# Rank-16 corrections on TensorE's row groups: 80 columns of the third chunk move from row groups 2 and 3 to 0 and 1, behind a semaphore

## The chip, the core and the metric

The kernel runs on one core of one Trainium2 chip. The metric is the device time of one execution in microseconds (us); the time before is the median of three runs. The profiles are of one further execution each, taken by the hardware profiler.

## The reference, cut to what matters

4096 tokens (128 batches of 32) of 512 features go through two layers. Each batch picks its own rank-16 adapter by an index.

```
# layer 0, for batch b with adapter i = itok_B_2_6[b], F = 1376
gate = x @ W_gate.T + 0.5 * (x @ A_gate[i].T) @ B_gate[i].T
up   = x @ W_up.T   + 0.5 * (x @ A_up[i].T)   @ B_up[i].T
act  = silu(gate) * up
down = act @ W_down.T + 0.5 * (act @ A_down[i].T) @ B_down[i].T
x    = x + down @ sign(weight).T + bias0
# layer 1, for batch b with adapter j = itok_B_4_50[b]
x    = x + ffn1(cond1(x, A[j], B[j]))      # linear, with low-rank parts
```

The change is in the terms `(x @ A[i].T) @ B[i].T` of gate and up, 1376 columns each, contracted over 16 ranks.

## The kernel before, in words

**Tiling.** The tokens are worked in 32 steps of 128 tokens, which are 4 batches of 32. A step is software-pipelined: step g computes gate and up of tile g, the down product of tile g-1 (`prev`) and layer 1 of tile g-2 (`pp`). Gate and up are cut into three chunks of columns, `CHUNKS`: the narrow one of 352, and two of 512. Each chunk has two PSUM banks, one for gate and one for up: `GU_BANK = [(4, 5), (0, 1), (2, 3)]`. The big products run in the full 128x128 array in split precision (three products for one).

**The rank-16 products.** They have a contraction of only 32 rows (two batches of 16 ranks), and an output of 64 tokens (the same two batches), so each uses a tile of 32 rows and 64 columns of TensorE's array. The array has four row groups of 32 rows, and two halves of 64 columns: eight such tiles. Index n (0 or 1) is the pair of batches and picks the half of 64 columns; r (0 to 3) is the row group, and the operands have to lie in the partitions of that row group. `b_rows` holds the adapters' B: in row groups 0 and 1 the gate and up parts of the first chunk (352 columns) and behind it those of the second chunk (512); in row groups 2 and 3 only the third chunk's 512 columns at that second place. `lhs_sb` holds the small left operands, and `lhs2_sb` its rows of groups 0 and 1 copied into the partitions of groups 2 and 3.

`first_rows` (L910) issues, per n, a layer-1 product into `out_ps` (L894, row group 2, 512 columns), a down correction into `y_ps` (L898, row group 3, 512 columns), and gate and up of the narrow chunk (L918, row groups 0 and 1, 352 columns). Its last product raises the semaphore `first_mm`. `second_rows` (L922) issues, per n, four products of 512 columns (L927): the second chunk's gate and up on row groups 0 and 1, the third chunk's on 2 and 3. Its last raises `second_mm`.

**What sets the order.** The program of each engine is written out by hand and runs in that order, with semaphores between engines. In `step` (L932) TensorE runs gate and up of the three chunks, the small products in between, then `first_rows`, `second_rows`, then `down` (L836, 33 products of 128x512) for the tile before, and then the next step. ScalarE (ACT) waits for `first_mm` before the narrow chunk's silu and for `second_mm` before the other two (L464). Step 0 has no `out_ps`, `y_ps` or `down` products, step 1 has no `out_ps` products. `load_b` (L322) brings `b_rows` of the next tile on SyncE's queue (SP), 4 transfers a step.

Each fp32 product here appears as two passes in the trace: 8 products of L927 per step times 32 steps are 256, and the trace has 512. The two passes of a product are called A and B below.

Of the kernel before, what the change touches and what calls it, by code (L numbers as in the profile page):

```python
# [18 lines left out]
CHUNKS = [(1024, 352), (0, 512), (512, 512)]  # L19
# [14 lines left out]
T_AT, TD_AT, T1_AT = 0, T_W, T_W + TD_W  # L34
SMALL = T_W + 2 * TD_W
LORA_ROWS = 4 * RANK
PAIR = CHUNKS[0][1] + CHUNKS[1][1]
ROW = 3 * 512
LINE = 512
GU_BANK = [(4, 5), (0, 1), (2, 3)]  # L40
# [35 lines left out]
PAIRS = GB // 2  # L76


def build_adaln_ffn(nc, xT, x, wgu, signT, wd, bd, btab, atab, la, lbw, w1T, a1, b1tab, b1end,
                    bias, ids, consts, sb_table, c_table, out):  # L80
    ctx = ExitStack()
    with ctx:

        base = (nc.sbuf_base + LINE - 1) // LINE * LINE
        cursor = [base]

        def place(name, shape, dtype, at=None, line=LINE):
            n = 4 * int(np.prod(shape[1:]))
            n = (n + line - 1) // line * line
            if at is None:  # L90
                at = cursor
            t = nc.alloc_sbuf_tensor_at(name, shape, dtype, offset=at[0])
            at[0] += n
            return t
# [15 lines left out]
        lhs_sb = place("lhs_sb", [P, P], f32)  # L110
        lhs2_sb = place("lhs2_sb", [P, P], f32)
        loop_at = [cursor[0]]
        b_rows = place("b_rows", [P, PAIRS, PAIR], f32)
        cs_rows = place("cs_rows", [P, PAIRS, H], f32)
# [7 lines left out]
        actT_sb = place("actT_sb", [P, NBLK, 2, P], f32r)  # L122
        ad_raw = place("ad_raw", [P, GB, ADW], f32)
        b1_raw = place("b1_raw", [P, GB, KC * RANK], f32)
        cursor[0] += 12288
        loop_end = cursor[0]
        bias_sb = place("bias_sb", [P, 2, H], f32)
        const_sb = place("const_sb", [P, CONST_W], f32, line=32)
# [40 lines left out]
        def bank(name):  # L169
            return ctx.enter_context(nc.psum_tensor(name, [P, 512], f32))  # L170

        gu_ps = [bank(f"gu{n}_ps") for n in range(6)]
# [7 lines left out]
        def sem(name):  # L180
            return ctx.enter_context(nc.semaphore(name))
# [14 lines left out]

        names = ("xT_in", "xT_hi", "xT_lo", "xT_used", "x_in", "x_biased", "x1_done", "x1_turned", "x1T_in", "x1_biased",
                 "out_done", "stored", "a_in", "ad_moved", "b1_in", "b_in", "c_in", "sbd_in", "small_mm", "small_scaled",
                 "lhs_ready", "lhs2_in", "first_mm", "second_mm", "y_mm", "silu_done", "act_done", "act_turned",
                 "act_in0", "act_in1", "act_in2", "actT_hi", "actT_lo")  # L200
        L = {n: sem(n) for n in names}
        names = ("x1_half", "x1_tr", "x1_raw", "b1_in", "c_in", "lhs_ready", "x1_biased")
# [35 lines left out]
        def group(r):  # L238

            return slice(r * QUAD, (r + 1) * QUAD)  # L240
# [5 lines left out]
        def pair(n):  # L246

            return slice(n * 2 * SEQ, (n + 1) * 2 * SEQ)
# [546 lines left out]
        def _(pe):  # L795
# [9 lines left out]
            def gate(g, c, pieces=range(KC)):  # L805
                f, w = CHUNKS[c]
                if 0 in pieces:
                    if c == 0:
                        if first(g):
                            pe.wait_ge(S["wg_lo"], KC)  # L810
                        pe.wait_ge(L["xT_lo"], g + 1)
                    if not first(g):
                        pe.wait_ge(L["act_done"], g * NC - NC + c + 1)
                product(gu_ps[GU_BANK[c][0]][:, 0:w], [(xT_sb[:, k, a, :], wg_sb[:, b, k, f:f + w])
                                                       for k in pieces for a, b in THREE], None,
                        start=0 in pieces, stop=KC - 1 in pieces)

            def up(g, c, pieces=range(KC)):
                f, w = CHUNKS[c]
                if 0 in pieces and first(g):  # L820
                    pe.wait_ge(S["wu_lo"], (c + 1) * KC)
                last = product(gu_ps[GU_BANK[c][1]][:, 0:w], [(xT_sb[:, k, a, :], wu_sb[:, b, k, f:f + w])
                                                              for k in pieces for a, b in THREE], None,
                               start=0 in pieces, stop=KC - 1 in pieces)
                if c == NC - 1 and KC - 1 in pieces:
                    last.then_inc(L["xT_used"], 1)

            def down(g, c, to=y_ps, blocks=range(4), begin=False):
                if 0 in blocks:
                    pe.wait_ge(L["actT_lo"], g * NC + c + 1)  # L830
                count = len(CHUNK_BLOCKS[c])
                for n, blk in enumerate(CHUNK_BLOCKS[c]):
                    if n not in blocks:
                        continue
                    for a, b in THREE:
                        last = nc.tensor.matmul(to[:], actT_sb[:, ACTT_SLOT[c] + n, a, :], down_sb[:, blk, b, :],  # L836
                                                start=begin and (c, n) == (0, 0) and (a, b) == (0, 0),
                                                stop=c == NC - 1 and n == count - 1 and (a, b) == (1, 0),
                                                skip_group_check=True)
                return last  # L840
# [30 lines left out]
            def small_ready(g, prev, pp):  # L871
                pe.wait_ge(L["a_in"], 16 * GB * (g + 1))
                if first(g):
                    pe.wait_ge(S["down_lo"], NBLK)
                if prev is not None:
                    pe.wait_ge(L["act_in0"], SENT * g)
                    pe.wait_ge(L["act_in1"], SENT * g)
                    pe.wait_ge(L["act_in2"], SENT * g)
                    pe.wait_ge(L["ad_moved"], g)
                if pp is not None:  # L880
                    pe.wait_ge(L["x1T_in"], SENT * (pp + 1))
                    pe.wait_ge(L["b1_in"], 16 * GB * (pp + 1))
                    after(pe, L["out_done"], pp)

            def small(prev, pp):
                last = t_rows()
                if prev is not None:
                    last = td_rows()
                if pp is not None:
                    last = t1_rows(b1_raw)  # L890
                last.then_inc(L["small_mm"], 1)
# [9 lines left out]
            def lora_ready(g, prev, pp):  # L901
                pe.wait_ge(L["lhs2_in"], g + 1)
                pe.wait_ge(L["b_in"], 16 * GB * (g + 1))
                if prev is not None:
                    pe.wait_ge(L["sbd_in"], 16 * GB * g)
                    after(pe, L["x1_done"], prev)
                if pp is not None:
                    pe.wait_ge(L["c_in"], 16 * GB * (pp + 1))

            def first_rows(prev, pp):  # L910
                w = CHUNKS[0][1]
                for n in range(PAIRS):
                    if pp is not None:
                        out_rows(n)
                    if prev is not None:
                        down_rows(n)
                    for u in range(2):
                        last = nc.tensor.matmul(gu_ps[GU_BANK[0][u]][pair(n), 0:w], lhs_sb[group(u), pair(n)],  # L918
                                                b_rows[group(u), n, 0:w], start=False, stop=True, skip_group_check=True)
                last.then_inc(L["first_mm"], 1)  # L920

            def second_rows():  # L922
                for n in range(PAIRS):
                    for r in range(4):
                        c, u = 1 + r // 2, r % 2
                        lhs = lhs_sb if c == 1 else lhs2_sb
                        last = nc.tensor.matmul(gu_ps[GU_BANK[c][u]][pair(n), :], lhs[group(r), pair(n)],  # L927
                                                b_rows[group(r), n, CHUNKS[0][1]:PAIR], start=False, stop=True,
                                                skip_group_check=True)
                last.then_inc(L["second_mm"], 1)  # L930

            def step(g, prev, pp):  # L932
                gate(g, 0)
                up(g, 0)
                gate(g, 1)
                up(g, 1, range(0, 1))
                small_ready(g, prev, pp)
                up(g, 1, range(1, 2))
                small(prev, pp)
                up(g, 1, range(2, 4))  # L940
                gate(g, 2)
                up(g, 2, range(0, 3))
                lora_ready(g, prev, pp)
                up(g, 2, range(3, 4))
                first_rows(prev, pp)
                second_rows()
                if prev is not None:
                    for c in range(NC):
                        down(prev, c).then_inc(L["y_mm"], 1)
# [95 lines left out]
            for n, blk in enumerate(BLOCK_ORDER):  # L1045
# [5 lines left out]
                else:  # L1051
                    pe.wait_ge(S["down_lo"], n - 3)
                product(ring_ps[(KC + 10 + n) % 4][:], [(half[:, k, at], sign_sb[:, k, :])
                                                             for k in range(KC) for half in (wd_hi, wd_lo)],
                        S["down_mm"])
            step(0, None, None)
            step(1, 0, None)
            step(2, 1, 0)
            with pe.Fori(3, G - 1) as g:
# [62 lines left out]
```

## Time and profile before

| | |
|---|---|
| Runs | 904.69, 906.72, 906.94 us; median 906.72 us |
| Profiled execution, span from the first to the last instruction | 904.5 us; its own time is given only by this span |
| TensorE matmul (PE) busy | 896.3 us, 99% of the span |
| TensorE weight load (PEld) busy | 723.2 us |
| VectorE (DVE), ScalarE (ACT), GpSimd (POOL) busy | 411.8, 200.6, 100.2 us |
| Chain that ended last | PE 94% |
| One step of the loop | 26.15 us |

In the profile's rows, a time is in microseconds from the span's start, and L with a number is the line of the kernel. PE is TensorE's matrix products, PEld its loading of weights, which overlaps PE. The end of a matmul is modelled: it lies later than the moment at which the last column went in. "Idle before" is the time an engine sat idle, and behind the arrow stands what released it. SPq and ACTq are the DMA queues of SyncE and ScalarE.

### The profile page before, as it was taken

How to read it: one execution, taken by the hardware profiler on the slowest of the kernel's cores; microseconds unless marked ns; L12 is line 12 of the kernel's file. 1: busy time of each engine (PE TensorE's matmuls, PEld its weight loads, DVE VectorE, ACT ScalarE, POOL GpSimd, SP SyncE). 2: the span in 40 equal slices, each digit the busy share in tenths (PEclk: the TensorE clock that was granted, in tenths of full speed). 3: DMA queues.
4: the chain of work that ended last, by engine and by line, in shares of the span. 5: the costliest groups of instructions: out<-in, count | busy, mean ns of one | idle time of the engine just before them, and what ended most of it. 6: DMA issues, size and time to landing. Idle time of an engine off the chain costs nothing.

```text
span 904.5 us, 25718 instructions
## 1 busy us (share of the span) xinstructions
PE 896.3 (99%) x9487; PEld 723.2 (80%) x9487; DVE 411.8 (46%) x1021; ACT 200.6 (22%) x349; POOL 100.2 (11%) x79
## 2 busy tenths in 40 slices
PE   8999999999999999999999999999999999999998
PEld 5887788778888887888888788888887888888775
DVE  5853435444353444534444444353544434444444
ACT  4852212112112111111212212121211211211110
POOL 0200111010111110101111010111100011111011
PEclk9999999999999999999999999999999999999999
DMA  9925454554554455545455555554555545445533
GB/s 336 418 97 146 122 144 132 147 141 138 144 145 135 129 147 147 142 131 152 131 135 143 148 141 133 151 136 139 133 146 144 142 136 148 134 133 144 148 109 88
DMA packets 147413, 134.71 MB, mean 149 GB/s; under 512 B 53312, under 2 KB 118848, under 8 KB 147264
## 3 DMA queue, kind: packets, MB, share of 16 engines
q1 hardware_dynamic: 92160, 108.59, 41.5%
q10 hardware_dynamic: 54288, 22.70, 9.7%
q0 software_dynamic: 944, 3.15, 0.9%
q8 instruction: 13, 0.21, 0.1%
q14 instruction: 8, 0.07, 0.0%
HBM read 92.14 MB, written 11.01 MB: 114 GB/s over the span
## 4 chain that ended last, share of the span: by engine, by line
PE 94%; SPq 2%; DMA 1%; issue 1%; DVE 1%; ACT 0%; DVEq 0%; ACTq 0%
PE gu_ps L799 54%; PE y_ps L836 26%; PE gu_ps L927 3%; PE out_ps L856 3%; PE out_ps L894 2%; PE out_ps L845 1%; PE y_ps L799 1%; PE out_ps L866 1%; PE out_ps L799 1%; PE gu_ps L918 1%; SPq L256 1%; DMA a_raw<-in_a 1%; SPq L313 0%; SPq L343 0%; SPq L350 0%
## 5 line engine op out<-in xcount | busy, mean ns | idle before, releaser
L799 PE MATMUL gu_ps<-wu_sb,xT_sb 128*128 128x512 f32 (+1 forms) x1152 | 261.4, 371 | 0.5 <-DMA landed<-act_sb 0.3
L799 PE MATMUL gu_ps<-wg_sb,xT_sb 128*128 128x512 f32 (+1 forms) x1152 | 251.9, 367 | 0.4 <-DVE act_sb L620 0.4
L836 PE MATMUL y_ps<-down_sb,actT_sb 128*128 128x512 f32 x1023 | 241.6, 393 | 0.0
L836 PEld LDWEIGHTS y_ps<-down_sb,actT_sb 128*128 128x128 f32 x1023 | 189.6, 188 | 64.0 <-issue 25.2
L799 PEld LDWEIGHTS gu_ps<-wg_sb,xT_sb 128*128 128x128 f32 x1152 | 206.9, 188 | 31.6 <-DVE xT_sb L602 1.3
L799 PEld LDWEIGHTS gu_ps<-wu_sb,xT_sb 128*128 128x128 f32 x1152 | 204.3, 188 | 30.1 <-issue 1.2
L602 DVE TENSOR_TENSOR actT_sb<-landed,actT_sb 128x512 fp32r<-128x512 f32 (+1 forms) x96 | 61.5, 642 | 198.6 <-ACT actT_sb L455 198.6
L455 ACT CAST actT_sb<-landed 128x512 fp32r<-128x512 f32 (+1 forms) x96 | 56.1, 585 | 307.7 <-issue 273.1
L643 DVE STREAM_TRANSPOSE lhs_sb<-t_own 32x32 f32<-32x32 f32 x512 | 103.9, 203 | 7.7
L425 POOL TENSOR_TENSOR x_in<-x_in,bias_sb 128x512 f32<-128x512 f32 x32 | 41.4, 1293 | 592.8 <-DMA x_in<-in_x 592.8
L602 DVE TENSOR_TENSOR xT_sb<-xT_raw,xT_sb 128x512 fp32r<-128x512 f32 x32 | 22.1, 692 | 124.7 <-ACT xT_sb L455 124.7
L429 POOL TENSOR_TENSOR x_sb<-x_sb,bias_sb 128x512 f32<-128x512 f32 x31 | 51.2, 1651 | 166.4 <-DVE x_turn L655 166.4
L634 DVE TENSOR_TENSOR t_own<-out_ps,const_sb 128x128 f32<-128x128 f32 (+3 forms) x35 | 9.8, 280 | 124.4 <-PE out_ps L866 119.6
L624 DVE STREAM_TRANSPOSE act_sb<-act_sb 128x512 f32<-128x512 f32 (+1 forms) x96 | 64.1, 667 | 3.3
L620 DVE TENSOR_TENSOR act_sb<-act_sb,gu_ps 128x512 f32<-128x512 f32 (+1 forms) x96 | 58.0, 604 | 0.2 <-ACT act_sb L466 0.2
L455 ACT COPY ad_raw<-a_raw 128x704 f32<-128x704 f32 x32 | 25.0, 782 | 146.3 <-PE out_ps L866 139.4
L466 ACT ACTIVATE act_sb<-gu_ps 128x512 f32<-128x512 f32 (+1 forms) x96 | 49.7, 552 | 29.0 <-PE gu_ps L918 19.5
L927 PE MATMUL gu_ps<-b_rows,lhs_sb 32*64 32x512 f32 x512 | 42.6, 588 | 0.0
L455 ACT CAST xT_sb<-xT_raw 128x512 fp32r<-128x512 f32 x32 | 19.8, 620 | 94.3 <-PE gu_ps L799 94.3
L894 PE MATMUL out_ps<-cs_rows,lhs_sb 32*64 32x512 f32 (+1 forms) x128 | 34.5, 606 | 0.0
L898 PE MATMUL y_ps<-cs_rows,lhs_sb 32*64 32x512 f32 x124 | 33.9, 613 | 0.0
L856 PE MATMUL out_ps<-ad_raw,landed 128*32 128x16 f32 x2816 | 31.4, 185 | 0.0
(121 smaller groups left out, 475.1 us busy)
## 6 DMA issues: line engine op xcount, KB each, us to landing
b_rows<-in_btab SPq DMA_DIRECT2D x128, 216.0 KB
a_raw<-in_atab SPq DMA_DIRECT2D x128, 152.0 KB, 2.4
landed<-act_sb SPq DMA_DIRECT2D x132, 64.0 KB, 2.1
xT_raw<-in_xT SPq DMA_DIRECT2D x32, 256.0 KB, 2.6
x_in<-in_x SPq DMA_DIRECT2D x32, 256.0 KB, 2.8
landed<-act_sb ACTq DMA_DIRECT2D x124, 64.0 KB, 2.2
x_landed<-x_turn ACTq DMA_DIRECT2D x124, 64.0 KB, 2.2
out_x<-out_sb SPq DMA_DIRECT2D x31, 256.0 KB, 2.9
```

The costliest lines, as they stand in the source:

```text
L429: nc.gpsimd.tensor_tensor(x1_sb[:], x1_sb[:], bias_sb[:, 1, :], ALU.add).then_inc(L["x1_biased"], 1)
L455: return nc.scalar.copy(o, i)
L466: nc.scalar.activation(act_sb[c][:, 0:w], gu_ps[GU_BANK[c][0]][:, 0:w], ACT.Silu).then_inc(L["silu_done"], 1)
L602: return nc.vector.tensor_tensor(o, whole, hi(high), ALU.subtract)
L620: nc.vector.tensor_tensor(a, a, gu_ps[GU_BANK[c][1]][:, 0:w], ALU.mult).then_inc(L["act_done"], 1)
L624: nc.vector.transpose(act_sb[c][:], act_sb[c][:]).then_inc(L["act_turned"], 1)
L643: turned = nc.vector.transpose(lhs_sb[group(group_of[r]), tokens(b)], wide[tokens(b), :])
L799: last = nc.tensor.matmul(o, w, m, start=start and n == 0, stop=stop and n == len(terms) - 1, skip_group_check=not check)
L836: last = nc.tensor.matmul(to[:], actT_sb[:, ACTT_SLOT[c] + n, a, :], down_sb[:, blk, b, :], start=begin and (c, n) == (0, 0) and (a, b) == ...
L856: last = nc.tensor.matmul(small_ps[tokens(b), TD_AT:TD_AT + TD_W], landed[c][:, at:at + SEQ], ad_raw[:, b, blk * RANK:(blk + 1) * RANK], s ...
L894: return nc.tensor.matmul(to[pair(n), at], lhs_sb[group(r), pair(n)], cs_rows[group(r), n, at], start=True, stop=True, skip_group_check=True)
L927: last = nc.tensor.matmul(gu_ps[GU_BANK[c][u]][pair(n), :], lhs[group(r), pair(n)], b_rows[group(r), n, CHUNKS[0][1]:PAIR], start=False, s ...
```

## The change

`HEAD` is 432 and `TAIL` is 80. The third chunk's last 80 columns of gate and up are stored behind the second chunk's in row groups 0 and 1 of `b_rows`, which grows from 864 to 944 columns (`PAIR`); the free space behind the loop's tiles shrinks by 512 bytes per partition. Four new products (`tail_rows`) compute these 80 columns on row groups 0 and 1, between `first_rows` and `second_rows`. They write the banks that the third chunk's products of row groups 2 and 3 write. Therefore the last of them raises a new semaphore `tail_mm`, for which TensorE itself waits. `second_rows` now issues the second chunk's four products first, then waits, then issues the third chunk's four, of 432 columns.

```diff
-PAIR = CHUNKS[0][1] + CHUNKS[1][1]
+HEAD = 432
+TAIL = CHUNKS[2][1] - HEAD
+LOW = CHUNKS[0][1] + CHUNKS[1][1]
+PAIR = LOW + TAIL
...
-        cursor[0] += 12288
+        cursor[0] += 11776
...
-            def second_rows():
+            def tail_rows():
+
                 for n in range(PAIRS):
-                    for r in range(4):
-                        c, u = 1 + r // 2, r % 2
-                        lhs = lhs_sb if c == 1 else lhs2_sb
-                        last = nc.tensor.matmul(gu_ps[GU_BANK[c][u]][pair(n), :], lhs[group(r), pair(n)],
-                                                b_rows[group(r), n, CHUNKS[0][1]:PAIR], start=False, stop=True,
+                    for u in range(2):
+                        last = nc.tensor.matmul(gu_ps[GU_BANK[2][u]][pair(n), HEAD:HEAD + TAIL],
+                                                lhs_sb[group(u), pair(n)], b_rows[group(u), n, LOW:PAIR],
+                                                start=False, stop=True, skip_group_check=True)
+                last.then_inc(L["tail_mm"], 1)
+
+            def second_rows(g):
+                w = CHUNKS[0][1]
+                for n in range(PAIRS):
+                    for u in range(2):
+                        nc.tensor.matmul(gu_ps[GU_BANK[1][u]][pair(n), :], lhs_sb[group(u), pair(n)],
+                                         b_rows[group(u), n, w:LOW], start=False, stop=True, skip_group_check=True)
+                pe.wait_ge(L["tail_mm"], g + 1)
+                for n in range(PAIRS):
+                    for u in range(2):
+                        last = nc.tensor.matmul(gu_ps[GU_BANK[2][u]][pair(n), 0:HEAD], lhs2_sb[group(2 + u), pair(n)],
+                                                b_rows[group(2 + u), n, w:w + HEAD], start=False, stop=True,
                                                 skip_group_check=True)
                 last.then_inc(L["second_mm"], 1)
...
                 first_rows(prev, pp)
-                second_rows()
+                tail_rows()
+                second_rows(g)
...
             to = 0 if c == 0 else CHUNKS[0][1]
+            if c == 2:
+                b_rows[:, u, :, LOW:PAIR] = part[:, :, f + HEAD:f + w]
+                w = HEAD
             b_rows[:, u + (2 if c == 2 else 0), :, to:to + w] = part[:, :, f:f + w]
```

The new lines move the numbers of the lines behind them: L894 becomes L897, L898 L901, L918 L921, L836 L839; the tail products stand in L929, the second chunk's in L938 and the third's in L943.

TensorE (PE), in the loop's body, from the first of `first_rows` to the first `down` product, before:

```order
L894 MATMUL out_ps<-cs_rows,lhs_sb 64x512
L898 MATMUL y_ps<-cs_rows,lhs_sb 64x512
L918 MATMUL gu_ps<-b_rows,lhs_sb 64x352 x2
L894 MATMUL out_ps<-cs_rows,lhs_sb 64x512
L898 MATMUL y_ps<-cs_rows,lhs_sb 64x512
L918 MATMUL gu_ps<-b_rows,lhs_sb 64x352 x2
L927 MATMUL gu_ps<-b_rows,lhs_sb 64x512 x8
L830 ISA
L836 MATMUL y_ps<-down_sb,actT_sb 128x512 [waits actT_lo]
```

The same place after the change:

```order
L897 MATMUL out_ps<-cs_rows,lhs_sb 64x512
L901 MATMUL y_ps<-cs_rows,lhs_sb 64x512
L921 MATMUL gu_ps<-b_rows,lhs_sb 64x352 x2
L897 MATMUL out_ps<-cs_rows,lhs_sb 64x512
L901 MATMUL y_ps<-cs_rows,lhs_sb 64x512
L921 MATMUL gu_ps<-b_rows,lhs_sb 64x352 x2
L929 MATMUL gu_ps<-b_rows,lhs_sb 64x80 x4
L938 MATMUL gu_ps<-b_rows,lhs_sb 64x512 x4
L943 MATMUL gu_ps<-b_rows,lhs_sb 64x432 [waits tail_mm]
L943 MATMUL gu_ps<-b_rows,lhs_sb 64x432 x3
L833 ISA
L839 MATMUL y_ps<-down_sb,actT_sb 128x512 [waits actT_lo]
```

Eight products of 512 have become four of 80, four of 512 and four of 432, and the first of the last four waits. Nothing else moved here. Step 0 on TensorE, before, with the last full-array product of `up` ahead and the next step's first behind:

```order
L799 MATMUL gu_ps<-wu_sb,xT_sb 128x512 [waits b_in,lhs2_in]
L799 MATMUL gu_ps<-wu_sb,xT_sb 128x512 x2
L918 MATMUL gu_ps<-b_rows,lhs_sb 64x352 x4
L927 MATMUL gu_ps<-b_rows,lhs_sb 64x512 x8
L799 MATMUL gu_ps<-wg_sb,xT_sb 128x352 [waits act_done,xT_lo]
```

and after the change:

```order
L802 MATMUL gu_ps<-wu_sb,xT_sb 128x512 x2
L921 MATMUL gu_ps<-b_rows,lhs_sb 64x352 x4
L929 MATMUL gu_ps<-b_rows,lhs_sb 64x80 x4
L938 MATMUL gu_ps<-b_rows,lhs_sb 64x512 x4
L943 MATMUL gu_ps<-b_rows,lhs_sb 64x432 [waits tail_mm]
L943 MATMUL gu_ps<-b_rows,lhs_sb 64x432 x3
L802 MATMUL gu_ps<-wg_sb,xT_sb 128x352 [waits act_done,xT_lo]
```

In step 0 row groups 2 and 3 have no earlier product; here too the third chunk's products now stand behind the wait.

## Rows read from the trace of the kernel before

**Rows 1.** The page: busy time by engine, and TensorE's granted clock in 40 slices.

```profile
PE 896.3 (99%) x9487; PEld 723.2 (80%) x9487; DVE 411.8 (46%) x1021; ACT 200.6 (22%) x349; POOL 100.2 (11%) x79
...
PEclk9999999999999999999999999999999999999999
```

**Rows 2.** The chain that ended last, 404 to 415 us: start, length, what.

```profile
405.80 0.86 PE gu_ps L927 x16
406.66 7.72 PE y_ps L836 x33
```

**Rows 3.** Groups by line: busy us, mean ns, idle before.

```profile
L927 PE MATMUL gu_ps<-b_rows,lhs_sb 32*64 32x512 f32 x512 | 42.6, 588 | 0.0
L927 PEld LDWEIGHTS gu_ps<-b_rows,lhs_sb 32*64 32x64 f32 x512 | 19.8, 132 | 7.3
```

**Rows 4.** Timeline, one loop step's row-group products: start, length, engine, line, count, idle before.

```profile
404.70 0.64 PE L894 MATMUL out_ps<-cs_rows,lhs_sb 32*64 32x512 f32 x1
404.71 0.64 PE L898 MATMUL y_ps<-cs_rows,lhs_sb 32*64 32x512 f32 x1
404.71 0.51 PE L918 MATMUL gu_ps<-b_rows,lhs_sb 32*64 32x352 f32 x2
...
405.18 0.59 PE L894 MATMUL out_ps<-cs_rows,lhs_sb 32*64 32x512 f32 x1
...
405.21 0.59 PE L898 MATMUL y_ps<-cs_rows,lhs_sb 32*64 32x512 f32 x1
405.36 1.30 PE L927 MATMUL gu_ps<-b_rows,lhs_sb 32*64 32x512 f32 x16
406.59 0.30 PEld L836 LDWEIGHTS y_ps<-down_sb,actT_sb 128*128 128x128 f32 x2 [0.81 <-issue]
```

**Rows 5.** Timeline of PE at 405.3 to 405.4 us: L918's B passes, L927's first.

```profile
405.06 0.49 PE L918 MATMUL gu_ps<-b_rows,lhs_sb 32*64 32x352 f32 x4
...
405.36 0.62 PE L927 MATMUL gu_ps<-b_rows,lhs_sb 32*64 32x512 f32 x4
```

**Rows 6.** Timelines of PE at 406.0 to 406.1 and 406.25 to 406.3 us.

```profile
405.61 1.05 PE L927 MATMUL gu_ps<-b_rows,lhs_sb 32*64 32x512 f32 x12
...
405.79 0.87 PE L927 MATMUL gu_ps<-b_rows,lhs_sb 32*64 32x512 f32 x8
```

**Rows 7.** Timeline, a later small product of 32 columns on 32-column weights.

```profile
422.26 0.46 PE L845 MATMUL out_ps<-a_raw,xT_raw 128*32 128x32 f32 x32
```

**Rows 8.** Timeline of ACT in the same step: the silus that wait for first_mm and second_mm.

```profile
406.00 0.46 ACT L466 ACTIVATE act_sb<-gu_ps 128x352 f32<-128x352 f32 x1 [0.52 <-PE gu_ps L918]
406.75 1.09 ACT L466 ACTIVATE act_sb<-gu_ps 128x512 f32<-128x512 f32 x2 [0.28 <-PE gu_ps L927]
```

**Rows 9.** Timeline of step 0, where no out_ps or y_ps product runs.

```profile
71.68 0.53 PE L918 MATMUL gu_ps<-b_rows,lhs_sb 32*64 32x352 f32 x4
...
72.03 0.47 PE L918 MATMUL gu_ps<-b_rows,lhs_sb 32*64 32x352 f32 x4
...
72.20 1.16 PE L927 MATMUL gu_ps<-b_rows,lhs_sb 32*64 32x512 f32 x12
...
72.57 0.46 ACT L466 ACTIVATE act_sb<-gu_ps 128x352 f32<-128x352 f32 x1
```

**Rows 10.** Timeline near the end: VectorE's step, and the weight load that waits for it.

```profile
886.95 0.65 DVE L602 TENSOR_TENSOR actT_sb<-landed,actT_sb 128x512 fp32r<-128x512 f32 x1
...
887.65 0.99 PEld L836 LDWEIGHTS gu_ps<-down_sb,actT_sb 128*128 128x128 f32 x5 [0.48 <-DVE actT_sb L602]
```

**Rows 11.** Timeline of SP's queue, and the transfers by line (KB each).

```profile
419.61 3.38 SPq L326 DMA_DIRECT2D b_rows<-in_btab  x4
...
b_rows<-in_btab SPq DMA_DIRECT2D x128, 216.0 KB
```

**Rows 12.** One step as a window: busy time and records of each engine, clock, DMA share, GB/s.

```profile
404.70:430.85 26.15, 26.15 (x290) 21.29 (x289) 11.54 (x30) 5.00 (x9) 2.94 (x2) 1.00 0.51 141
```

More of the change, by code:

```diff
@@ L198, in build_adaln_ffn @@
                  "out_done", "stored", "a_in", "ad_moved", "b1_in", "b_in", "c_in", "sbd_in", "small_mm", "small_scaled",
-                 "lhs_ready", "lhs2_in", "first_mm", "second_mm", "y_mm", "silu_done", "act_done", "act_turned",
+                 "lhs_ready", "lhs2_in", "first_mm", "second_mm", "tail_mm", "y_mm", "silu_done", "act_done", "act_turned",
                  "act_in0", "act_in1", "act_in2", "actT_hi", "actT_lo")
```

## Prediction, made before the changed kernel ran

> **What bounds the kernel now.** I read the page first: TensorE is busy for 896.3 of 904.5 us and its granted clock stands in the top tenth in every slice [rows 1], and a loop step shows clock 1.00 and TensorE busy for all of its 26.15 us [rows 12]. So no clock effect is in play, and whatever lengthens or shortens TensorE's own row of work shows in the end 1 to 1. The chain of waits says the same where the change sits: L927 runs straight into the 33 down products, with nothing between [rows 2]. By group, L927 costs 42.6 us of TensorE's time [rows 3], or 1.33 us a step. But these are up to eight products at a time, and a mean of 588 ns tells nothing of who ends last. The timeline of one step does, cut into narrow windows so that it shows the four-product groups apart.
>
> All eight tiles of the array start together at 404.70 [rows 4]. A pass goes by its columns: L918's B passes (352 columns) start at 405.06 and the next product on their row groups at 405.36 [rows 5], 0.30 us; L927 on row groups 0 and 1 starts its A passes at 405.36 [rows 5], and its B passes at 405.79 [rows 6], 0.43 us for 512 columns. Both are 0.84 ns a column. The first pass after the change of tile shape costs 0.05 us more (L894 from 404.70 to 405.18 is 0.48, against 0.43) [rows 4]: there nothing hid its weight load. So, with "in" for the moment at which the last column has gone in:
>
> - row groups 0 and 1: 352 then 512; in at 405.79 + 0.43 = 406.22.
> - row groups 2 and 3: 512 then 512; the third chunk's A passes start at 405.61 [rows 6], and are in at 405.61 + 0.86 = 406.47. They end last, 0.25 us behind the others.
>
> The down products' weights start at 406.59 [rows 4], 0.12 us after that. This switch of tile shape stays.
>
> **The change part by part.**
>
> *Columns.* Groups 2 and 3 lose 80 columns per n, in two passes: 160 x 0.84 = 0.13 us. Groups 0 and 1 gain them: tail A passes at 405.36, B at 405.43, the second chunk's A at 405.50, its B at 405.93, in at 406.36. An 80-column pass (0.067 us) must also hide the next weight load. What a load occupies is less than the 0.13 us of its record [rows 3]: L845's 32 passes over four column tiles take 0.46 us, of which about 0.2 is the last one's modelled tail, so 8 per tile in 0.26, 0.03 us for 32 columns of weights [rows 7]; 64 columns are then some 0.05 to 0.06, just under 0.067. If a load did occupy all its 0.13 us, each of the two tail passes would last 0.06 us longer, and groups 0 and 1 would be in at 406.49; by the next point they still don't end last. I cost this at nothing.
>
> *The wait.* This is the term that decides. Without it the columns alone would bring the end from 406.47 to 406.36, 0.11 us a step. The third chunk's first weight load may now start only when `tail_mm` has been seen. When is that? The last tail pass starts about 405.46 and its record would end 0.07 + 0.16 us later (0.16 is a record's length less its columns: 0.59 - 0.43), at 405.69. But a semaphore of TensorE seems to be raised in program order, after every earlier product is complete. `first_mm` shows it. It hangs on L918's last, whose records end at 405.06 + 0.49 = 405.55 [rows 5], and ScalarE, idle for 0.52 us and waiting for just that, starts only at 406.00 [rows 8]: 0.45 us later. In step 0, where L894 and L898 don't run, L918's records end at 72.03 + 0.47 = 72.50 and ScalarE starts at 72.57 [rows 9]: 0.07 us. For `second_mm` it is 406.75 [rows 8] less 405.36 + 1.30 = 406.66 [rows 4]: 0.09 us. What is issued ahead of L918's last and ends behind it is L898's B pass on the other half, at 405.21 + 0.59 = 405.80 [rows 4]. From there to 406.00 is 0.20 us, of which some is ScalarE's own step before its instruction. `tail_mm` stands behind the same L898, and eight more passes. So the signal can't come before 405.80, and TensorE's waking adds what it does elsewhere: VectorE ends at 887.60 and the weight load starts at 887.65 [rows 10], 0.05 us. Bounds: 405.80 + 0.09 = 405.89 if it is as prompt as `second_mm`, and 406.00 + 0.08 = 406.08 if it is later than ScalarE's start on `first_mm` by 0.01 us for each of the eight tail passes behind. I take 405.98, nearer to what `first_mm` shows, since the same backlog stands ahead of it.
>
> The Trainium skill (TensorE: Matmul & The Clock Gate, Part 3, "The mechanism") says that matmuls start and end strictly in program order. By this trace half of it fails: L918's B passes start at 405.06, ahead of L894's at 405.18 [rows 4, 5], although L894 is issued first. The half on the end is what `first_mm` shows. Taken whole, it would hold the third chunk's start until the second chunk's B passes have started, at 405.93 to 405.96, and the sum would be within 0.02 us of the same.
>
> *The third chunk's end.* Its weight load is exposed now, as for L894: 0.05 us. Then two passes of 432 columns, 0.72 us: 405.98 + 0.05 + 0.72 = 406.75, against 406.47. That is +0.28 us a step. Row groups 0 and 1, in at 406.36, wait for it. Queued behind the waiting load on TensorE are the 33 down products and the next step, all on the path; nothing gives the time back, as TensorE is idle nowhere in a step [rows 12]. The silus of the second and third chunk wait for `second_mm` and come 0.28 us later, but so does everything that uses them, so no new wait arises. The narrow chunk's silu doesn't move.
>
> *Step 0.* L918 starts at 71.68, and the second and third chunk on their tiles are in at about 71.68 + 0.05 + 0.60 + 0.86 = 73.19. After: the tail ends at 71.68 + 0.05 + 0.60 + 0.13 + 0.16 = 72.62, plus 0.09 and 0.05 to 72.76, plus 0.05 + 0.72 = 73.53: +0.34 us.
>
> *Transfers.* `b_rows` grows from 864 to 944 columns, 9%, so 216 KB becomes 236 KB, four times a step. They are issued from 419.61 to 422.99 [rows 11], and the next step's row-group products, which use them, begin at 430.85 [rows 12], 7.9 us later; 9% of a transfer of a few us, with the DMA engines at 0.51, fits in that gap: nothing. The four more products (8 more passes) add no time on TensorE's issue, as eight products started within 0.05 us of each other at 404.70.
>
> *Sum.* 31 x 0.28 + 0.34 = 9.0 us. The profiled execution's span would go from 904.5 to 913.5. The median of the runs is 2.2 us above that span, so 906.7 + 9.0 = 915.7; I give 915.5.
>
> **The rivals.**
>
> 1. *The signal comes with the tail's own completion.* Then it is at 405.69, the load starts at 405.69 + 0.09 = 405.78, and the third chunk is in at 406.55: +0.08 us a step, 2.7 us, 909.4. For it: the tail's tiles are done by then. Against it: the 0.45 us of `first_mm`, against 0.07 without the longer products.
> 2. *The balance pays: faster.* The wait is released before it binds. The third chunk is in before 406.47 only if its load starts before 405.69, and the full 0.11 us a step comes if it starts by 405.58. Then 32 x -0.11 = -3.5 us, 903.2. For it: the two pairs of row groups are unequal by 0.25 us now. Against it: the tail's records themselves end at 405.69, so even a signal without any delay gives nothing.
> 3. *TensorE drains at the wait.* The waiting load holds back until the second chunk's products are done, or these are held with it: the third chunk starts at 406.36 and is in at 407.13, +0.66 us a step, 21 us, 927.8. For it: no wait on a product that is still running in the array is in the trace. Against it: passes start ahead of earlier-issued ones on other tiles, so tiles don't hold each other back; and the second chunk is issued ahead of the wait.
> 4. *No difference*, the wait being absorbed by idle time elsewhere: there is none in a step, and this is worth 906.7.
>
> **How the numbers follow.** Forecast 0.80, rival 1 0.07, rival 2 0.03, rival 3 0.07, rival 4 0.03. The forecast's own range is from the load's start at 405.89 (+0.19, 6.1 us, 912.8) to 406.08 (+0.38, 12.1 us, 918.8). The runs before spread over 2.2 us, and so I take the range from 909.2, which lets rival 1 in, to 919.5. Left out are rivals 2, 3 and 4. A measurement here can tell about 0.3%, or 2.7 us, from no change. Rival 1 falls on that bound, and I give half of it to each side. Faster 0.03; same 0.03 + 0.04 = 0.07; slower 0.90.
>
> **What would show it.** In the changed profile: a step's period of 26.43 us in place of 26.15; the third chunk's first weight load (L943) some 1.28 us after the step's first L897 (405.98 - 404.70), where the third chunk's first pass before was at 0.91; a gap of about 0.37 us on row groups 2 and 3 between the end of L897's and L901's B passes and that start; tail passes 0.07 us apart; the first down weights at 2.17 us after the first L897, in place of 1.89; the narrow chunk's silu still 1.30 us after it. I am wrong if L943 starts at 1.08 or earlier (rival 1), if it starts only at 1.66 (rival 3), or if the down products don't move.

## The result

The changed kernel takes 914.46 us (median of 4 runs, 914.19 to 915.03), the kernel before 905.76 us in the same comparison (median of 4 runs, 904.69 to 906.94; the 906.72 us that I predicted from was the median of three of them): a ratio of 1.0098, 95% interval 1.0082 to 1.0114. It is slower by 8.7 us. A later comparison gave 914.97 against 905.96 us, 1.0099 (1.0078 to 1.0119). I predicted 915.5 us, in a range from 909.2 to 919.5.

### The profile page after: what moved, and what is told of

Same layout as the page of the kernel before. It is cut to its first block, busy times and chain, and to the rows that moved or that the text cites. A ratio compares the mean times of both kernels' runs of the same rounds, so it can differ in the third digit from the quotient of the medians.

```text
span 912.5 us, 26230 instructions
## 1 busy us (share of the span) xinstructions
PE 905.4 (99%) x9743; PEld 725.2 (79%) x9743; DVE 414.8 (45%) x1021; ACT 200.9 (22%) x349; POOL 99.9 (11%) x79
## 4 chain that ended last, share of the span: by engine, by line
PE 95%; SPq 2%; DVE 1%; issue 1%; DMA 1%; ACT 0%; DVEq 0%
PE gu_ps L802 54%; PE y_ps L839 25%; PE out_ps L859 3%; PE gu_ps L938 3%; PE out_ps L897 2%; PE gu_ps L943 2%; PE out_ps L848 1%; PE y_ps L802 1%; PE out_ps L802 1%; PE gu_ps L921 1%; PE out_ps L869 1%; SPq L259 1%; DVE act_sb L627 0%; PE gu_ps L929 0%; DVE act_sb L623 0%
## 5 line engine op out<-in xcount | busy, mean ns | idle before, releaser
L839 PE MATMUL y_ps<-down_sb,actT_sb 128*128 128x512 f32 x1023 | 241.1, 393 | 0.0
L839 PEld LDWEIGHTS y_ps<-down_sb,actT_sb 128*128 128x128 f32 x1023 | 189.6, 188 | 59.5 <-issue 21.0
L897 PE MATMUL out_ps<-cs_rows,lhs_sb 32*64 32x512 f32 (+1 forms) x128 | 34.5, 606 | 0.0
L859 PE MATMUL out_ps<-ad_raw,landed 128*32 128x16 f32 x2816 | 34.0, 186 | 0.0
L901 PE MATMUL y_ps<-cs_rows,lhs_sb 32*64 32x512 f32 x124 | 33.9, 613 | 0.0
L938 PE MATMUL gu_ps<-b_rows,lhs_sb 32*64 32x512 f32 x256 | 33.6, 587 | 0.0
```

The costliest lines, as they stand in the source:

```text
L859: last = nc.tensor.matmul(small_ps[tokens(b), TD_AT:TD_AT + TD_W], landed[c][:, at:at + SEQ], ad_raw[:, b, blk * RANK:(blk + 1) * RANK], s ...
L897: return nc.tensor.matmul(to[pair(n), at], lhs_sb[group(r), pair(n)], cs_rows[group(r), n, at], start=True, stop=True, skip_group_check=True)
L938: nc.tensor.matmul(gu_ps[GU_BANK[1][u]][pair(n), :], lhs_sb[group(u), pair(n)], b_rows[group(u), n, w:LOW], start=False, stop=True, skip_g ...
```

## The profile after

The page has TensorE as busy as before, and the clock as full [rows 1]; the step shown here takes 26.46 us, against 26.15 [rows 12] (the means over the loop's steps are 26.45 and 26.15):

```profile
span 912.5 us, 26230 instructions
...
PE 905.4 (99%) x9743; PEld 725.2 (79%) x9743; DVE 414.8 (45%) x1021; ACT 200.9 (22%) x349; POOL 99.9 (11%) x79
...
PEclk9999999999999999999999999999999999999999
```

```profile
407.66:434.12 26.46, 26.46 (x304) 21.37 (x304) 11.64 (x30) 5.00 (x9) 2.95 (x2) 1.00 0.53 142
```

The second is the window of one step, with the columns of [rows 12]. This is the same place as [rows 4], in the timeline of PE:

```profile
407.66 0.64 PE L897 MATMUL out_ps<-cs_rows,lhs_sb 32*64 32x512 f32 x1
...
408.14 0.59 PE L897 MATMUL out_ps<-cs_rows,lhs_sb 32*64 32x512 f32 x1
...
408.17 0.59 PE L901 MATMUL y_ps<-cs_rows,lhs_sb 32*64 32x512 f32 x1
408.32 0.33 PE L929 MATMUL gu_ps<-b_rows,lhs_sb 32*64 32x80 f32 x8
408.45 1.05 PE L938 MATMUL gu_ps<-b_rows,lhs_sb 32*64 32x512 f32 x8
409.00 0.95 PE L943 MATMUL gu_ps<-b_rows,lhs_sb 32*64 32x432 f32 x8
409.88 0.97 PE L839 MATMUL y_ps<-down_sb,actT_sb 128*128 128x512 f32 x3
```

and in those of the weight loads (PEld) and of ACT:

```profile
408.39 0.23 PEld L938 LDWEIGHTS gu_ps<-b_rows,lhs_sb 32*64 32x64 f32 x8
408.99 0.21 PEld L943 LDWEIGHTS gu_ps<-b_rows,lhs_sb 32*64 32x64 f32 x8 [0.37 <-PE gu_ps L929]
409.88 0.76 PEld L839 LDWEIGHTS y_ps<-down_sb,actT_sb 128*128 128x128 f32 x4 [0.68 <-issue]
```

```profile
408.96 0.47 ACT L469 ACTIVATE act_sb<-gu_ps 128x352 f32<-128x352 f32 x1 [0.52 <-PE gu_ps L921]
410.02 1.09 ACT L469 ACTIVATE act_sb<-gu_ps 128x512 f32<-128x512 f32 x2 [0.59 <-PE gu_ps L943]
```

Read from the step's first product (407.66, and 404.70 in [rows 4]): the tail's records end at 408.32 + 0.33 = 408.65, 0.99 after it, where the prediction has 405.69, also 0.99. The third chunk's first weights come at 408.99, 1.33 after it, 0.34 us behind those records. The down weights come at 2.22, against 1.89 before. The narrow chunk's silu stands where it was, at 1.30 [rows 8]. The summary of waits names the place in 31 steps:

```profile
PEld gu_ps L943 <- PE gu_ps L929: 11.5, 31, 0.4
```

Row groups 2 and 3, free at 0.91, stand still until 1.33.

## The experiments

Positions are from the step's first row-group product, a step's length is the mean over the loop's steps in the trace. Theory: a semaphore of TensorE is raised in program order, so `tail_mm` waits for the longer products issued ahead of the tail, on other row groups.

**1. The tail ahead of everything.** Nothing long stands ahead of `tail_mm` here, and the wait is kept.

```diff
-                first_rows(prev, pp)
                 tail_rows()
+                first_rows(prev, pp)
                 second_rows(g)
```

> The changed kernel with tail_rows ahead of first_rows, wait kept. Theory (TensorE's semaphore is raised in program order, behind the longer out_ps and y_ps products): nothing long stands ahead of tail_mm now, it comes about 0.45 us after the step's first product, before row groups 2 and 3 are free at 0.91; the wait costs nothing and the balanced columns pay: both pairs of row groups are in at 1.64, against 1.77 in the kernel before, step 26.02 us in place of 26.15, 31 steps x -0.13 = -4.0 us, about 901.7 us against 905.8. Rival (a wait inside the row-group products costs a fixed drain or wake of 0.3 us wherever its signal comes from): the third chunk still starts at about 1.3, step 26.4 us, about 914 us.

Measured: 901.4 us against 905.53, ratio 0.9952 (0.9938 to 0.9965); step 26.02 us. Its PE and PEld timelines:

```profile
481.28 0.30 PE L929 MATMUL gu_ps<-b_rows,lhs_sb 32*64 32x80 f32 x4
...
482.22 0.56 PE L943 MATMUL gu_ps<-b_rows,lhs_sb 32*64 32x432 f32 x4
482.49 0.61 PE L938 MATMUL gu_ps<-b_rows,lhs_sb 32*64 32x512 f32 x4
482.58 0.55 PE L943 MATMUL gu_ps<-b_rows,lhs_sb 32*64 32x432 f32 x4
```

```profile
481.79 0.17 PEld L943 LDWEIGHTS gu_ps<-b_rows,lhs_sb 32*64 32x64 f32 x4
...
483.06 0.30 PEld L839 LDWEIGHTS y_ps<-down_sb,actT_sb 128*128 128x128 f32 x2 [0.68 <-issue]
```

The waiting weights are loaded at 0.51, beside the products before them, and the third chunk starts at 0.94, as soon as its row groups are free. Both pairs are in together: 482.49 + 0.43 = 482.92 and 482.58 + 0.36 = 482.94. The wait itself costs nothing once its signal is early. The rival of a fixed price of 0.3 us falls: the trace records the rise of `tail_mm` at 0.41, and the waiting weights are loaded 0.10 us behind it.

**2. The long products behind the tail.** The tail stays behind the narrow chunk; the `out_ps` and `y_ps` products are issued after it.

```diff
                 for n in range(PAIRS):
-                    if pp is not None:
-                        out_rows(n)
-                    if prev is not None:
-                        down_rows(n)
                     for u in range(2):
...
                 first_rows(prev, pp)
                 tail_rows()
+                wide_rows(prev, pp)     # out_rows and down_rows; its last raises first_mm
                 second_rows(g)
```

> The changed kernel with the out_ps and y_ps products issued behind the narrow chunk's and the tail's, ahead of the second chunk's; first_mm is raised by the last y_ps product. Theory (program order): only the tail's own products stand before tail_mm, so it comes at their own completion, 0.985 + 0.04 = 1.03 us after the first product; the third chunk's weights start at 1.07 in place of 1.33, down weights 2.21 - 0.26 = 1.95, step 26.19 to 26.22 us, about 907 to 908.5 us. Rival (the signal was late because of something else than the out_ps and y_ps products, such as the short passes or the wait itself): third chunk still at 1.33, step 26.44 us, 914.5 us.

Measured: 905.47 us against 905.53, ratio 0.9995 (0.9986 to 1.0004); step 26.15 us. The timelines of PE and PEld:

```profile
482.92 0.53 PE L917 MATMUL gu_ps<-b_rows,lhs_sb 32*64 32x352 f32 x4
...
483.56 0.32 PE L935 MATMUL gu_ps<-b_rows,lhs_sb 32*64 32x80 f32 x8
```

```profile
483.96 0.21 PEld L949 LDWEIGHTS gu_ps<-b_rows,lhs_sb 32*64 32x64 f32 x8
484.85 0.30 PEld L839 LDWEIGHTS y_ps<-down_sb,actT_sb 128*128 128x128 f32 x2 [0.68 <-issue]
```

The tail's records end at 483.56 + 0.32 = 483.88, and the waiting weights follow 0.08 us later, at 1.04 in place of 1.33. The tail's passes are the same, at nearly the same place. Only what was issued ahead of them differs. The signal then comes with the tail's own completion. The weights stand 0.03 us ahead of what I expected, the down weights at 1.93 as expected (1.95), but the step is 0.04 to 0.07 us shorter than expected: it gives back what the place loses, behind the start of the down weights (see the end of the next section).

**3. The wait without the tail.** The kernel before, second chunk's products first, then a wait for `first_mm`, then the third chunk's, 512 columns each.

```diff
+                for c in (1, 2):
+                    if c == 2:
+                        pe.wait_ge(L["first_mm"], g + 1)
                     for n in range(PAIRS):
-                    for r in range(4):
-                        c, u = 1 + r // 2, r % 2
+                        for u in range(2):
+                            r = u + (2 if c == 2 else 0)
```

> The kernel before, columns unchanged (no tail), with the second chunk's four products issued ahead of the third's, and between them a wait of TensorE for its own first_mm. Theory (program order): the third chunk's weights start at first_mm 1.20 + 0.04 = 1.24 us, and two passes of 512 are in at 2.15 against 1.77: +0.38 us a step, step 26.53 us, +11.8 us, about 917.5 us. If the signal came with the narrow chunk's own completion (0.85 + 0.04): weights at 0.93, +0.07 us a step, 908 us. If the cost in the changed kernel came from the tail's passes and not from the wait: no change, 905.8 us.

Measured: 917.14 us against 905.53, ratio 1.0119 (1.0099 to 1.0139); step 26.48 us. The timeline of PEld:

```profile
541.93 0.13 PEld L894 LDWEIGHTS out_ps<-cs_rows,lhs_sb 32*64 32x64 f32 x1 [0.35 <-issue]
...
543.17 0.21 PEld L930 LDWEIGHTS gu_ps<-b_rows,lhs_sb 32*64 32x64 f32 x8 [0.42 <-PE gu_ps L918]
544.19 0.30 PEld L836 LDWEIGHTS y_ps<-down_sb,actT_sb 128*128 128x128 f32 x2 [0.81 <-issue]
```

The weights start at 1.24, as expected of program order, though the product that raises `first_mm` has its record's end at 0.85. So the tail isn't needed for the loss: with the late signal and the new order alone it is 11.6 us, and experiment 4 shows that the order costs nothing.

**4. The order without the wait.** The kernel before with the second chunk's four products first.

```diff
+                for c in (1, 2):
                     for n in range(PAIRS):
-                    for r in range(4):
-                        c, u = 1 + r // 2, r % 2
+                        for u in range(2):
+                            r = u + (2 if c == 2 else 0)
```

> The kernel before with the second chunk's four products issued ahead of the third's and no wait. Theory (tiles start as soon as they are free, whatever was issued ahead on other tiles): no change, step 26.15 us, 905.8 us. Rival (products start in program order): the third chunk's A passes can't start before the second chunk's B passes at 1.09 to 1.12, in place of 0.91: +0.2 us a step, step 26.35 us, about 912 us.

Measured: 906.05 us against 905.53, ratio 1.0005 (0.9993 to 1.0018); step 26.14 us, the down weights at 1.89:

```profile
535.68 0.13 PEld L894 LDWEIGHTS out_ps<-cs_rows,lhs_sb 32*64 32x64 f32 x1 [0.35 <-issue]
...
537.57 0.30 PEld L836 LDWEIGHTS y_ps<-down_sb,actT_sb 128*128 128x128 f32 x2 [0.81 <-issue]
```

That is the timeline of PEld. The one of PE, cut to 537.00 to 537.02 us, when the second chunk's A passes are over, shows the third chunk's A passes and the second chunk's B passes:

```profile
536.59 0.80 PE L928 MATMUL gu_ps<-b_rows,lhs_sb 32*64 32x512 f32 x8
```

The third chunk starts at 0.91, as before the edit, and the second chunk's B passes, issued ahead of it, can't start before 1.09. The new order costs nothing: products of different tiles start when their tile is free.

**5. The tail in twice as many products.** Each tail product of 80 columns is two of 40, so 16 passes stand between `first_mm` and `tail_mm`.

```diff
                     for u in range(2):
-                        last = nc.tensor.matmul(gu_ps[GU_BANK[2][u]][pair(n), HEAD:HEAD + TAIL],
+                        for at in (0, TAIL // 2):
+                            last = nc.tensor.matmul(gu_ps[GU_BANK[2][u]][pair(n), HEAD + at:HEAD + at + TAIL // 2],
...
```

> The changed kernel with each tail product of 80 columns split into two of 40: 16 tail passes between first_mm and tail_mm in place of 8. In the changed kernel tail_mm is raised 0.093 us after first_mm. Theory a (completions behind the long products are worked off one by one, 0.012 us a pass): tail_mm comes 0.19 us after first_mm, the third chunk's weights start at 1.42 in place of 1.33, step 26.53 us, 31 x 0.09 = 2.8 us above the changed kernel, about 917.3 us. Theory b (0.093 us is what a second semaphore costs, whatever stands between): third chunk at 1.33, step 26.44 us, 914.5 us. Under both, row groups 0 and 1 end later by 0.09 us at most and don't end last.

Measured: 915.62 us against 905.96, ratio 1.0104 (1.0083 to 1.0126); step 26.46 us. The timelines of PE and PEld:

```profile
541.66 0.59 PE L897 MATMUL out_ps<-cs_rows,lhs_sb 32*64 32x512 f32 x1
...
542.04 0.62 PE L940 MATMUL gu_ps<-b_rows,lhs_sb 32*64 32x512 f32 x1
542.05 0.24 PE L930 MATMUL gu_ps<-b_rows,lhs_sb 32*64 32x40 f32 x2
542.29 0.80 PE L940 MATMUL gu_ps<-b_rows,lhs_sb 32*64 32x512 f32 x4
```

```profile
541.18 0.13 PEld L897 LDWEIGHTS out_ps<-cs_rows,lhs_sb 32*64 32x64 f32 x1 [0.35 <-issue]
...
542.59 0.21 PEld L945 LDWEIGHTS gu_ps<-b_rows,lhs_sb 32*64 32x64 f32 x8
543.47 0.30 PEld L839 LDWEIGHTS y_ps<-down_sb,actT_sb 128*128 128x128 f32 x2 [0.68 <-issue]
```

The weights come at 1.40 in place of 1.33 (the mean over the loop's steps; the rounded rows give 542.59 - 541.18 = 1.41): eight more passes ahead of the signal cost 0.07 us, a little under 0.01 us each. That speaks for the backlog being worked off pass by pass, at less than the 0.012 us that I had. A fixed price of a second semaphore would have left 1.33. The time itself can't tell the two apart (0.65 us between the medians), and the step of 26.46 us isn't 26.53: again the rest of the step gives part of it back.

**6. The changed kernel again,** on the same chip as experiments 5 and 7.

```diff
(no edit to the changed kernel)
```

> The changed kernel as it is, on the same chip as the split one: 914.5 us against 905.5, step 26.44 us.

Measured: 914.97 us against 905.96; step 26.47 us. It reproduces.

**7. The tail first, with 48 columns.** Experiment 1 with `HEAD = 464`.

```diff
-HEAD = 432
+HEAD = 464
```

> As the kernel with tail_rows ahead of first_rows, but 48 columns moved in place of 80. Theory (the wait is free there, and columns cost 0.84 ns each): row groups 2 and 3 end last, at 0.94 + 2 x 0.39 = 1.72 against 1.66 with 80 and 1.77 before; down weights at 1.84, step 26.06 us, 902.9 us (31 x 0.05 above the 80-column version). Rival (the gain of that version comes from the new order and not from the balance): as with 80 columns, 901.4 us.

Measured: 902.26 us against 905.96, ratio 0.9957 (0.9940 to 0.9973); step 26.05 us against 26.02 of experiment 1. The timelines of PE and PEld:

```profile
482.82 0.27 PE L929 MATMUL gu_ps<-b_rows,lhs_sb 32*64 32x48 f32 x4
...
484.01 0.61 PE L938 MATMUL gu_ps<-b_rows,lhs_sb 32*64 32x512 f32 x4
484.14 0.58 PE L943 MATMUL gu_ps<-b_rows,lhs_sb 32*64 32x464 f32 x4
```

```profile
484.65 0.53 PEld L839 LDWEIGHTS y_ps<-down_sb,actT_sb 128*128 128x128 f32 x3 [0.73 <-issue]
```

Now row groups 2 and 3 end last again: 484.14 + 0.39 = 484.53 against 484.01 + 0.43 = 484.44, and the down weights come at 1.83, between 1.78 of experiment 1 and 1.89 before. In the trace the gain goes by the columns moved. In the times the two versions aren't apart, as their intervals overlap.

## Why the prediction was right, point by point

- **Which row groups end last, and 0.84 ns a column: right.** Experiments 1 and 7 place the down weights at 1.78 and 1.83 by this count. The balance was worth the 0.11 to 0.13 us a step that the columns give: 4.1 us in experiment 1.
- **The signal in program order: right.** It was argued from `first_mm` alone. Experiments 1 to 3 show it in three ways: with the tail first, with the long products behind it, and with no tail at all. Rival 1 (own completion) had the weights at 1.08; they come at 1.33, and at 1.04 only when nothing longer is issued ahead. The traces also record when each semaphore rises, and say the same directly. `first_mm` rises 0.35 us behind the end of its own product's record in a step of the kernel before (1.20 against 0.85), and 0.04 us behind it in step 0, where nothing longer is ahead. `tail_mm` rises 0.31 us behind (1.29 against 0.99) in the changed kernel, and 0.04 us behind in experiments 1 and 2. The waiting weights follow the rise by 0.04 us in the changed kernel and in experiments 2, 3 and 5.
- **The place of the signal: 0.05 us too early.** I took 405.98, that is 1.28; it is 1.33. I had counted 0.01 us for each tail pass behind `first_mm` in the upper bound, and then chosen a value below it. The backlog is near that bound: `tail_mm` rises 0.09 us after `first_mm` with 8 tail passes between them, and 0.16 us after it with the 16 of experiment 5. The bound I had set, 1.38, holds it.
- **Rival 3 (TensorE drains at the wait): wrong.** The third chunk's weights start at 408.99, while the second chunk's records run to 408.45 + 1.05 = 409.50. Its B passes start at 408.88, so that their last columns go in at 408.88 + 0.43 = 409.31, also behind that load.
- **Rival 2 (the balance pays): not in this order.** Its decision point was right: the load has to start before 0.99. Experiment 1 meets it, and is faster.
- **Step 0: wrong, +0.34 us predicted, nothing measured.** The third chunk is held as predicted: its weights start at 71.81, 1.05 after the first L921 at 70.76, where I had 1.08. But in step 0 nothing follows but the next step's gate product, and that waits for VectorE, which works on the narrow chunk. Before and after, in the timelines of step 0:

```profile
73.10 0.51 DVE L620 TENSOR_TENSOR act_sb<-act_sb,gu_ps 128x352 f32<-128x352 f32 x1
...
73.76 1.05 PE L799 MATMUL gu_ps<-wg_sb,xT_sb 128*128 128x352 f32 x5 [0.40 <-DVE act_sb L620]
```

```profile
70.76 0.82 PE L921 MATMUL gu_ps<-b_rows,lhs_sb 32*64 32x352 f32 x8
...
71.81 0.59 PE L943 MATMUL gu_ps<-b_rows,lhs_sb 32*64 32x432 f32 x4
...
72.18 0.51 DVE L623 TENSOR_TENSOR act_sb<-act_sb,gu_ps 128x352 f32<-128x352 f32 x1
...
72.84 0.40 PE L802 MATMUL gu_ps<-wg_sb,xT_sb 128*128 128x352 f32 x1
```

  The gate product starts 0.15 us behind VectorE's end in both, and 2.08 us behind the first L918 or L921 in both (71.68 to 73.76, 70.76 to 72.84). The 0.40 us of idle time was in the profile of before, and I had not looked there. After the change TensorE is busy for 2.00 of the same 2.08 us, so that 0.08 us of it is left.
- **The sum.** The two spans differ by 8.0 us. The work ahead of step 0's row-group products was 0.92 us shorter in this profile (70.76 against 71.68), in code that the change does not touch. From step 1 to step 31 it is these rows, of before and after:

```profile
90.77 0.64 PE L898 MATMUL y_ps<-cs_rows,lhs_sb 32*64 32x512 f32 x1
...
875.88 0.64 PE L894 MATMUL out_ps<-cs_rows,lhs_sb 32*64 32x512 f32 x1
```

```profile
89.82 0.64 PE L901 MATMUL y_ps<-cs_rows,lhs_sb 32*64 32x512 f32 x1
...
883.73 0.64 PE L897 MATMUL out_ps<-cs_rows,lhs_sb 32*64 32x512 f32 x1
```

  785.11 and 793.91 us, +8.80 over 30 steps, 0.293 us a step. I had 0.28. That mean mixes two things. The 27 steps from step 3 to step 30 grow by 0.30 us each, 8.1 us together. The other three (from steps 1, 2 and 30) change by -0.14, +1.17 and -0.32 us. The +1.17 is the step from 2 to 3, 25.98 us before and 27.15 after. It is not what the wait costs: in experiments 1 and 2, where the wait costs nothing or little, the same step takes 26.99 and 26.93 us. What sets it is not known.

  So it is in part luck that 915.5 lies only 1.0 us above the measured time. The place costs 0.05 us a step more than I had (31 x 0.05 = 1.6 us), the rest of the step gives 0.03 us back (0.9 us), the 0.34 us of step 0 isn't paid, and the time of before that I added to was 1.0 us above the median of the comparison.
- **What stays open.** The place itself has grown by 0.33 us in each step (down weights at 2.22 against 1.89), and a step by only 0.30 (26.45 against 26.15). In experiments 1, 2, 3, 5 and 7 the step is also shorter than the place says, by 0.03 to 0.08 us; in experiment 4, where the place doesn't move, by 0.01. The starts of the records, averaged over the 27 steps, show where. From the start of the first down product to that of the gate product behind them it is 7.63 us before, 7.62 in the changed kernel, 7.61 in experiment 2 and 7.59 in experiment 7. From the start of the first small product (L845 before) to that of the big product behind them it is 1.56 us before, 1.55 in the changed kernel, 1.54 in experiment 2, 1.53 in experiment 3 and 1.48 in experiment 5. The other stretches agree within 0.005 us. Why these two change I did not find, and no experiment was made on it.

## What to carry to other kernels

In these runs a TensorE semaphore reports every product issued before it, not only its own: `first_mm` and `tail_mm` rose 0.35 and 0.31 us behind their own products. So a product that others wait for belongs ahead of the long ones, even if it runs on other row groups. When work is spread over row groups, draw a line for each group with its columns, then add every wait as the time at which the *signal* is seen. Here the same edit gave +1.0% or -0.5% by one line's place. Before a cost is put on a step that differs from the loop's (the first, the last), look at what ends the idle time behind it.

## What the runs showed of the hardware that was not expected

- Products start out of program order across tiles, and complete in order. In experiment 4 the third chunk's A passes start at 0.91, ahead of B passes that are issued earlier. The kernel before shows it for whole products: the second chunk's products of the second pair (n = 1) are issued behind the third chunk's of the first pair, and start at 405.38 (four records from 405.36 [rows 5]), against 405.61 [rows 6]. The Trainium skill (TensorE: Matmul & The Clock Gate, Part 3, "The mechanism") has matmuls in program order at start and end; these runs bear out the end and not the start.
- A wait on a weight load whose semaphore had already risen cost nothing: in experiment 1 `tail_mm` rises at 0.41 us and these weights are loaded at 0.51, during the products before them.
- From the end of the last record ahead of it to the waiting weights it is 0.08 us in experiment 2 (483.88 to 483.96), with nothing long ahead of the signal. Each pass that stands behind a late product adds some 0.01 us (0.09 us for the 8 of the changed kernel, 0.16 for the 16 of experiment 5).
- Splitting the tail did more than lengthen the backlog. In experiment 5 one of the second chunk's four first passes starts at 542.04, and the others only from 542.29, just after the record of L897's B pass ends (541.66 + 0.59 = 542.25). Their tiles had only the tail's last short passes before them, which start at 542.05 and a little after. At that moment the 16 passes of `first_rows`, the 16 of the tail and one of the second chunk had been started, and by order of completion only one was complete: 32 were open. In the changed kernel, with 8 tail passes fewer, there is no such gap. It looks like a bound on open passes. It was seen in this one kernel, and no run was made to test it.
